# Recurrent block and expert layer on eight cores: second normalization deferred into the next block, first normalization moved behind the output projection, two weight rings one slot shorter

## The reference

```python
def attn(x, W_in, conv_w, conv_b, W_gates, b_gates, forget_base, W_out):
    u = einsum('ntc,hc->nth', x, W_in)               # 1024 -> 2 x 1536
    gate, xh = split(u, 2)
    xh = causal_depthwise_conv(xh, conv_w, conv_b)   # 4 taps
    g = einsum('nth,gh->ntg', xh, W_gates) + b_gates # 1536 -> 2 x 1536
    forget, inp = split(g, 2)
    alpha = exp(-8 * softplus(forget_base) * sigmoid(forget))
    beta = sqrt(1 - alpha ** 2 + 1e-6)
    h = scan(alpha, beta * sigmoid(inp) * xh)        # h_t = alpha_t h_(t-1) + xs_t
    return einsum('nth,dh->ntd', gelu(gate) * h, W_out)

x = x + layernorm(attn(layernorm(x)))
x = x + layernorm(ffn(layernorm(x)))   # router, 8 experts computed densely, one shared expert
```

## Time and profile before

| | |
|---|---|
| timed runs | 5997.56 and 6105.65 us, median 6051.61 us |
| the profiled execution | 5547.6 us |
| its span on the slowest core | 5546.1 us |
| spans of the 8 cores | 5473.1 to 5546.1 us |
| mean granted TensorE clock, by core | 0.887 to 0.898 |
| busy on the slowest core | PE 74%, DVE 43%, ACT 22%, POOL 11% |
| chain that ended last | PE 65%, DVE 12%, ACT 10%, DMA 7% |

### The profile page before, as it was taken

One profiled execution on the slowest core, in us unless ns is written; L12 is line 12 of the kernel. 1 busy time (PEld: TensorE's weight loads), 2 busy tenths in 40 slices (PEclk: granted clock), 3 DMA queues, 4 the chain that ended last, 5 costly groups with the idle time before them and its releaser, 6 DMA issues.

```text
span 5546.1 us, 52349 instructions; the slowest of 8 cores (5473.1 to 5546.1 us)
## 1 busy us (share of the span) xinstructions
PE 4109.6 (74%) x16496; PEld 1629.7 (29%) x16496; DVE 2357.5 (43%) x3808; ACT 1229.3 (22%) x1779; POOL 630.3 (11%) x1187
## 2 busy tenths in 40 slices
PE   4565565556655764898888898885788888988885
PEld 1222222212212221333333333331333333333331
DVE  2433432422233234544445544445544455444443
ACT  1332341313222231211111211121211122111121
POOL 1010011111111110111111111110111111111110
PEclk8788788788878886999999999996999999999986
DMA  5353354435344430343333343330333333433331
GB/s 75 52 86 63 57 88 61 63 51 86 48 69 64 67 59 16 52 76 56 64 66 60 61 75 58 62 60 31 52 56 64 66 58 62 73 59 61 61 52 40
DMA packets 179707, 336.66 MB, mean 61 GB/s; under 512 B 19456, under 2 KB 39952, under 8 KB 179312
## 3 DMA queue, kind: packets, MB, share of 16 engines
q0 software_dynamic: 175280, 324.92, 36.4%
q1 hardware_dynamic: 4160, 8.39, 0.4%
HBM read 649.41 MB, written 8.39 MB: 119 GB/s over the span
## 4 chain that ended last, share of the span: by engine, by line
PE 65%; DVE 12%; ACT 10%; DMA 7%; issue 5%; DVEq 0%; POOL 0%; ACTq 0%; POOLq 0%
PE pb L165 65%; ACT bufA L902 4%; DMA wi<-wi_xh 3%; DMA wi<-wi_gate 2%; DVE sa L532 1%; DVE sa L517 1%; ACT L513 1%; ACT ssf L513 1%; DMA wg<-wgates 1%; ACT L566 1%; DMA wo<-wout 1%; DVE ssi L529 1%; DVE ssi L526 1%; ACT ssi L566 1%; ACT sa L583 1%
## 5 line engine op out<-in xcount | busy, mean ns | idle before, releaser
L165 PE MATMUL pb<-xn,wq 128*128 128x512 bf16 x9216 | 2064.1, 383 | 264.3 <-ACT bufA L902 264.3
L165 PEld LDWEIGHTS pb<-xn,wq 128*128 128x128 bf16 x9216 | 887.2, 98 | 1446.6 <-issue 485.1
L165 PE MATMUL pb<-sxh,wg 128*128 128x512 bf16 x2304 | 596.5, 422 | 318.8 <-ACT ssf L566 290.7
L165 PE MATMUL pb<-a_s,w2s 128*128 128x512 bf16 x2304 | 562.9, 409 | 123.8 <-DVE a_s L957 123.8
L902 ACT ACTIVATE bufA<-pb,c_b1g 128x512 f32<-128x512 f32 x256 | 175.9, 687 | 1678.3 <-PE pb L165 1678.3
L165 PE MATMUL pb<-sxnbf,wi 128*128 128x512 bf16 x1152 | 332.2, 438 | 285.9 <-DMA wi<-wi_gate 122.7
L907 DVE SCALAR_TENSOR_TENSOR bufA<-pb,c_b3g,bufA 128x512 f32<-128x512 f32 x256 | 192.2, 751 | 672.5 <-ACT bufA L902 672.5
L165 PEld LDWEIGHTS pb<-sxh,wg 128*128 128x128 bf16 x2304 | 238.1, 106 | 677.1 <-issue 478.9
L165 PEld LDWEIGHTS pb<-a_s,w2s 128*128 128x128 bf16 x2304 | 235.3, 104 | 443.0 <-issue 235.3
L936 DVE TENSOR_TENSOR bufA<-bufA,bufC 128x512 f32<-128x512 f32 x288 | 199.5, 693 | 241.3 <-ACT bufC L931 241.3
L931 ACT ACTIVATE bufC<-bufA 128x512 f32<-128x512 f32 x288 | 181.3, 629 | 467.4 <-DVE bufA L926 467.3
(11 more groups left out here) (147 smaller groups left out, 2963.4 us busy)
## 6 DMA issues: line engine op xcount, KB each, us to landing
wg<-wgates POOLq DMA_DIRECT2D x192, 384.0 KB, 5.4
wq<-w1g POOLq DMA_DIRECT2D x128, 256.0 KB, 4.5
wq<-w3g POOLq DMA_DIRECT2D x128, 256.0 KB, 5.2
wq<-w1l POOLq DMA_DIRECT2D x128, 256.0 KB, 6.2
wq<-w3l POOLq DMA_DIRECT2D x128, 256.0 KB, 7.0
w2s<-w POOLq DMA_DIRECT2D x128, 256.0 KB, 5.0
wi<-wi_xh POOLq DMA_DIRECT2D x96, 256.0 KB, 4.1
wi<-wi_gate POOLq DMA_DIRECT2D x48, 256.0 KB, 4.0
```

The lines of the kernel that those rows point to most:

```text
L165: t.matmul(o, l, r, start=s1, stop=s2),
```

## The change

`lngate` is split into three: `lngate_stats` (sum matmuls), `lngate_rows` (row operations on VectorE and ScalarE) and `lngate_bc` (broadcast matmuls). With these:

- The statistics of ln1 of a main block stay where they were, behind the next block's front. Its rows come at the head of the next block, and its broadcast and the 24 x1 operations behind the next block's `ph_wgates_mid`, ahead of `ph_wout`.
- The x load of the next block and its squares move from the head of a block to the place behind `ph_wgates_mid` (and behind x1).
- ln0 of the next block moves as a whole behind `ph_wout`, where only its tail was.
- `wg` has 2 slots instead of 3, `wo` 3 instead of 4.
- The first two L517 operations of a block also wait for the last statistics matmul that reads `sa2`.

```diff
-            wg = WStream([asb(f"wg{j}", [128, NC_H, 128], BF16) for j in range(3)], "wg", "wg")
-            wo = WStream([asb(f"wo{j}", [128, 4, 128], BF16) for j in range(4)], "wo", "wo")
+            wg = WStream([asb(f"wg{j}", [128, NC_H, 128], BF16) for j in range(2)], "wg", "wg")
+            wo = WStream([asb(f"wo{j}", [128, 4, 128], BF16) for j in range(3)], "wo", "wo")
...
             def ph_ln0_tail(st):
...
-                stats_done = st_state[st]["ln0_stats"]
+                stats_done = lngate_bcast(st_state[st]["ln0_st"], f"ln0_{st}")
...
+                    sg2 = [guard["sa2_sq"]] if (mi < 2 and "sa2_sq" in guard) else []
...
-                    lis = {kk: wo.load(d_wo2[pss * NC_H + kk]) for kk in range(4)}
+                    lis = {kk: wo.load(d_wo2[pss * NC_H + kk]) for kk in range(3)}
...
-                        if k + 4 < NC_H:
-                            lis[k + 4] = wo.load(d_wo2[pss * NC_H + k + 4])
+                        if k + 3 < NC_H:
+                            lis[k + 3] = wo.load(d_wo2[pss * NC_H + k + 3])
...
-            def ph_ln1_x1(st):
+            def ph_ln1_stats(st):
...
+            def ph_ln1_rows(st):
+                st_state[st]["ln1_rows"] = lngate_rows(
+                    st_state[st]["ln1_st"], f"ln1_{st}",
+                    (row_m, row_q, row_r, row_mr))
+
+            def ph_ln1_bcast_x1(st):
...
+                stats_done = lngate_bc(st_state[st]["ln1_rows"], f"ln1_{st}")
...
             for st in range(_nst):
                 main = st >= 4
+                if st - 1 >= 4:
+                    ph_ln1_rows(st - 1)
+                if main:
+                    ph_gate(st)
+                ph_wgates_mid(st)
+                if st - 1 >= 4:
+                    ph_ln1_bcast_x1(st - 1)
                 if st + 1 < _nst:
                     ph_xload(st + 1)
                 if main:
-                    ph_gate(st)
-                ph_wgates_mid(st)
+                    ph_wout(st)
                 if st + 1 < _nst:
                     ph_ln0_stats(st + 1)
-                if main:
-                    ph_wout(st)
-                if st + 1 < _nst:
                     ph_ln0_tail(st + 1)
                     ph_front(st + 1)
                 if main:
-                    ph_ln1_x1(st)
+                    ph_ln1_stats(st)
+            ph_ln1_rows(_nst - 1)
+            ph_ln1_bcast_x1(_nst - 1)
```

More of the change, by code:

```diff
@@ L247, in build_nc, with lngate_stats @@
         g_dma(c_sb2[:], d_sb2, tag="c")
-        def lngate(srcs, sqs, ten_after, tag, src_waits=None, sq_waits=None,
-                   banks=(4, 5, 6, 7), fp32=False, sq_gen=None):
+        def lngate_stats(srcs, sqs, tag, src_waits=None, sq_waits=None,
+                         banks=(4, 5, 6, 7), fp32=False, sq_gen=None):
             sb0, sb1, bb0, bb1 = banks
@@ L253, in lngate @@
             n = len(srcs) if srcs is not None else len(sqs)
[L254 to L261, removed]
+            for c in range(n):
+                w = list(src_waits[c]) if src_waits else []
+                t_mm(pb[sb0][0:1, :], onesv[:], srcs[c],
+                     start=(c == 0), stop=(c == n - 1),
+                     waits=(bank_wait(sb0) if c == 0 else []) + w,
+                     tag=f"{tag}sx")
             if sq_gen is not None:
@@ L264, in lngate @@
                 for c in range(n):
-                    gw = [("t", rel[c - 2])] if (c - 2) in rel else (
-                        list(sq_waits[c]) if sq_waits else [])
-                    ap = sq_gen(c, gw + (list(sq_waits[c]) if sq_waits and c >= 2 else []))
+                    gw = [("t", rel[c - 2])] if (c - 2) in rel else []
+                    ap = sq_gen(c, gw)
                     aw = [("a", S.n["a"])]
@@ L280, in lngate, with lngate_rows @@
                          tag=f"{tag}sq")
-            tcnt = S.n["t"]
-            inv = 1.0 / (128 * n)
-            v_op(lambda v: v.tensor_scalar(out=row_m[:], in0=pb[sb0][0:1, :],
+            return (S.n["t"], banks, 128 * n)
+        def lngate_rows(state, tag, rbufs, row_wait=None):
+            tcnt, (sb0, sb1, bb0, bb1), nfeat = state
+            r_m, r_q, r_r, r_mr = rbufs
+            inv = 1.0 / nfeat
+            rg = [guard["rows"]] if "rows" in guard2 else []
+            v_op(lambda v: v.tensor_scalar(out=r_m[:], in0=pb[sb0][0:1, :],
                                            scalar1=inv, scalar2=None, op0=OP.mult),
-                 waits=[("t", tcnt)], tag=f"{tag}m")
-            v_op(lambda v: v.tensor_scalar(out=row_q[:], in0=pb[sb1][0:1, :],
+                 waits=[("t", tcnt)] + (row_wait or []) + rg, tag=f"{tag}m")
+            v_op(lambda v: v.tensor_scalar(out=r_q[:], in0=pb[sb1][0:1, :],
                                            scalar1=inv, scalar2=None, op0=OP.mult),
@@ L371, in ph_ln0_stats @@
                 xw = [(pre[st]["xsem"], pre[st]["xld"]), ("c", wc)]
-                stats_done = lngate([sxbf[:, c, :] for c in range(NC_D)],
+                stt_ = lngate_stats([sxbf[:, c, :] for c in range(NC_D)],
                                     [ssqbf[:, c, :] for c in range(NC_D)],
-                                    None, f"ln0_{st}",
+                                    f"ln0_{st}",
                                     src_waits=[xw] + [[]] * (NC_D - 1),
                                     sq_waits=pre[st]["sq_v"])
-                st_state[st] = {"ln0_stats": stats_done}
+                st_state[st] = {"ln0_st": stt_}
             def ph_ln0_tail(st):
@@ L519, in midchain @@
                             in1=ssf[:, pp, :], op0=OP.mult, op1=OP.mult),
-                         waits=[al_done], tag=f"na2{st}")
+                         waits=[al_done] + sg2, tag=f"na2{st}")
                     return S.n["v"]
@@ L633, in sqg1 @@
                     return sa2[:, c % 2, :]
[L635 to L639, removed]
-                guard["sxnbf"] = ("t", st_state[st]["wi_done"])
+                st_state[st]["ln1_st"] = lngate_stats(
+                    [sao[:, c, :] for c in range(NC_D)], None, f"ln1_{st}",
+                    src_waits=[[evao_a]] + [[]] * (NC_D - 1),
+                    banks=(2, 3, 2, 3), fp32=True, sq_gen=sqg1)
+                guard["sa2_sq"] = ("t", st_state[st]["ln1_st"][0])
+                guard["sxnbf"] = ("t", st_state[st]["wi_done"])
+            def ph_ln1_rows(st):
[3 more added lines that the diff above has]
+            def ph_ln1_bcast_x1(st):
+                par = st % 2
+                T0 = st * ST
+                stats_done = lngate_bc(st_state[st]["ln1_rows"], f"ln1_{st}")
                 Tm = T0 - NT
```

40 lines of the change are left out of this document (27 added, 13 removed).

## The result

The changed kernel is slower by 1.8%: ratio 1.0182, 95% interval 1.0161 to 1.0203. The forecast was +94 us, +1.6%. Its absolute number, 6146 us, stands on the two timed runs shown before, some 500 us longer than the others, a length that later executions have when one die or both show a lower TensorE clock (about 0.8); executions without it take about 5,500 us before and 5,590 to 5,612 us after, and only these are compared.

A forecast was written before the change was run, and what follows sets the result against it. It took TensorE's waits in the attention part (loads, x1, ln0, the `wg` ring) as the bound. Its terms summed to +94 us, added to 6051.6 for 6146 us, +1.6%; its own range 6100 to 6190, with rivals 6020 to 6240.

The forecast's parts named there:

- Gate start: Before the gate matmuls of blocks 5 to 7: waits behind x load and x1 go, -91 us in all.
- x1 and x load before the projection: Ahead of the output projection: it waits for x1, +35 us in block 7, and `wo` loads behind x load, +44 in blocks 5, 6.
- Block 4: Ahead of block 4's projection: no x1 there and ln0 gone, so it starts at about W + 1, -24 us.
- W: The time at which a block's gate-weight (`wg`) matmuls end, from which the forecast counts the projection's start.
- ln0 behind the projection: After the projection in blocks 4 to 6: ln0's statistics, rows, broadcast and normalization follow bare, 22 us each, +66.
- Squares: Blocks 0 to 3, after the last channel pair: the x load's 8 squares come before ln0's rows, +4.9 us each, +20.
- `wg` with two slots: Gate-weight stages: +3.4 us at each of eight starts, +27, less 3 in block 0; steady period unchanged, bounds -100 and +64.
- g3 cold and g1 warm: Gate-weight stage: of a pair's four 12-matmul groups, third at 1.2 GHz, first at 2.4; period 20.3 us, today 20.4.
- The warm one: Rival, gate-weight stage: TensorE keeps 2.4 GHz through two short waits, period 17.8 us, 100 come back, total 6046; chance 0.17.
- The cold one: Rival, gate-weight stage: first and third groups at the low clock, load bound, period 22.0 us, total 6230; chance 0.28.
- `wo` with three slots: Output projection: a slot's 4.8 us round trip over three slots gives 1.6 a step against 1.4, 5 a block, +20.
- Front stages: Front-stage matmuls on `wi` in blocks 0 to 4: no change forecast, 0 us.

The follow-up runs named there:

- e5: Changed kernel with ln1's broadcast and x1 moved behind the next block's third gate tile; attention part ends at 2045.7 us (changed 2156.1), ratio 0.9961 to before.
- e6: Changed kernel with the projection's first three `wo` loads issued ahead of x1 and the x load; attention part ends at 2133.6 us (changed 2156.1).
- e1: Changed kernel with `wg` back at 3 slots and `wo` at 4; attention part ends at 2108.7 us (changed 2156.1), ratio 1.0062 to before.
- e9: Kernel before with only ln0's statistics, rows and broadcast moved behind the projection; attention part ends at 2051.7 us (before 2063.4), ratio 0.9957.
- e10: Kernel before with only `wg` cut to 2 slots; attention part ends at 2078.0 us (before 2063.4), ratio 1.0019.
- e2: Kernel before, order untouched, with `wg` at 2 slots and `wo` at 3; attention part ends at 2104.0 us (before 2063.4), no ratio.
- e3: Kernel before with only the x load and its squares moved behind the gate-weight stage; attention part ends at 2024.5 us (before 2063.4), no ratio.
- e7: Kernel before with x1 in the gate stage, x load and ln0 spread over gate-weight stage and projection; attention part ends at 1874.2 us (before 2063.4).

## Why the prediction was right

*Gate start, -91.* Right in place and size. The bound of +3 a block for Gelu behind the rows wasn't needed: the third tile waits for ScalarE (3.30), but no longer than it waited for its load in block 7 before (3.39), where the row operations were done before the gate began.

*x1 and x load before the projection, +35 and +44.* Right, and the largest finding of the study: e5 shows that this placement costs 110 against the one in the gate stage, e6 that 11 of it is the order of two loads in GpSimd's queue. The pattern was read from the earlier trace rows and came back in the same size.

*Block 4, -24.* Off by 3: the projection starts at W + 3.4, not W + 1. It starts at W both in e6, where its loads go ahead of the x load, and in e1, where the order is the changed one and the rings are long: it takes the x load and the short rings together.

*ln0 behind the projection, +66.* Right (+68); e9 shows that against the 24.6 gone ahead of it the move is worth -11.6.

*Squares, +20.* Right (+19.5).

*`wg` with two slots.* The stages grew by 25, forecast +24 with block 0, all of it at their starts, and e10 confirms 22 for the ring alone. That the steady period stays at 20.4 held (20.5), but not in the way written, so here the number is luck in part: I took g3 cold and g1 warm; the trace has both partly slow. Neither rival came true. The warm one needed 17.8 a period. The cold one, for which the rule on loop structure in "TensorE: Matmul & The Clock Gate" of the Trainium skill spoke, needed 22.0. The rule's direction shows: a wait for loads inside the loop did bring the lower clock (0.77 over the two groups behind it). Its price was within what ScalarE's chain hides.

*`wo` with three slots, +20.* Mis-sized: 27 (e2 27.3). The steady round trip was right (1.62 a step measured, 1.6 used), but the forecast took 24 x 0.2 from it; the starts of the passes and matmuls at the lower clock come on top, 1.7 a step over a whole projection (40.9 / 24 in e2, where a `wo` matmul took 443 ns in the mean; before 415).

*Front stages, 0.* Missed: -10 in blocks 0 to 4. I counted the x load out of the way in block 0's gate weights only; e3 shows that its old place goes with a longer front too. This and the gate stages (-2.8) nearly cancel with the last point (+7.5) and block 4 (+3), which is luck, and why the sum was closer (94 to 92.7) than its parts.

## What to carry to other kernels

When a step is deferred, look for a stage in which the engine that does it is idle and the bank it holds is free. x1 and the x load gained 91 us by leaving their old place and lost all of it in the new one, because the projection needs x1's bank and the load queue; three tiles into the gate stage x1 cost 6 us in three blocks. Read the order of the load queue as part of the program: one load that waits, or a large one, moves everything behind it. Before a ring is shortened, divide its round trip (release, issue, landing, use) by the slots left and compare with the step; where another chain is longer the loss is only at the stage's start (25 us over eight stages here).

## What the hardware showed that I had not expected

- Front stages with nothing changed in them take 238 to 249 us in sum over five blocks, depending on where a 1 MB load is issued (about 7 us, e3 and the comparison behind it; by what path stays open).
- After waits of 2.8 to 4 us, two groups of 12 matmuls took 7.0 us again and again (granted clock 0.77), where one wait of 6.70 gave 5.1 for one group and 2.6 for the next. Two waits of about half the length cost 2 x 1.7 us of slower matmuls, one long wait 2.5. Below that the length alone doesn't tell: behind a wait of 2.54 in e7 there was no loss, and of two waits of 2.37 in e6 one was followed by 5.46 and one by 7.03.
